# Relational layers of a graph network: scores, score weights and first value weights made while the rows are turned

## The reference, cut to what matters

```python
xr = jnp.einsum('nd,rdf->rnf', x, W)              # values of every relation
oi = xr[etype, dst]; oj = xr[etype, src]
alpha = jax.nn.leaky_relu(oi @ q + oj @ k, 0.2)
m = jax.ops.segment_max(alpha, dst, num_segments=n_nodes)
e = jnp.exp(alpha - m[dst])
z = jax.ops.segment_sum(e, dst, num_segments=n_nodes)
a = e / (z[dst] + 1e-16)
out = jax.ops.segment_sum((a[:, :, None] * oj.reshape(-1, heads, out_ch)).reshape(-1, heads * out_ch), dst, num_segments=n_nodes) + b
```

## Time and profile before

| | |
|---|---|
| median of the runs | 2976.41 us |
| the profiled execution: its time, its span | 2970.5 us, 2968.8 us |
| mean granted TensorE clock | 0.913 of full speed |
| PE, DVE, ACT, GpSimd busy | 2536.1, 2106.1, 1315.0, 310.4 us |
| layer 1: turning, scan, attention begin at | 1202.2, 1214.4, 1448.2 us |
| layer 2: turning, scan, attention begin at | 1866.6, 1879.1, 2096.8 us |

### The profile page before, as it was taken

How to read it: one execution, slowest core, us unless ns; L and a number is a source line. 1 busy time by engine, 2 the same in 40 slices (tenths; PEclk the granted TensorE clock), 3 DMA queues, 4 the chain that set the end, 5 groups by cost and what they waited for, 6 DMA issues and landing times. The chain is left out here.

```text
span 2968.8 us, 39008 instructions
## 1 busy us (share of the span) xinstructions
PE 2536.1 (85%) x14382; PEld 2118.7 (71%) x14383; DVE 2106.1 (71%) x3030; ACT 1315.0 (44%) x1649; POOL 310.4 (10%) x166
## 2 busy tenths in 40 slices
PE   6877894888856994799699999699999979998888
PEld 3556892232323994699699999599888769896668
DVE  6775899999974555699689988660567687136555
ACT  1573225989831000222578776221565563222431
POOL 0000000000003794000000000331000000000013
PEclk9997656999976997899899999899999999999989
DMA  2467542611104554455646643452634362311012
GB/s 69 131 174 180 150 150 67 237 52 35 35 33 178 189 197 158 154 180 160 201 121 181 170 118 90 150 171 81 187 122 129 102 194 70 85 54 59 1 41 80
DMA packets 174702, 366.47 MB, mean 123 GB/s; under 512 B 24871, under 2 KB 103541, under 8 KB 174034
## 3 DMA queue, kind: packets, MB, share of 16 engines
q1 hardware_dynamic: 122024, 274.54, 30.9%
q10 hardware_dynamic: 49312, 73.97, 7.4%
q0 software_dynamic: 3200, 15.73, 1.5%
HBM read 281.06 MB, written 83.12 MB: 123 GB/s over the span
## 5 line engine op out<-in xcount | busy, mean ns | idle before, releaser
L1649 PE MATMUL gat_acc<-far_u,gat_ft 125*65 125x512 f32 x720 | 286.3, 538 | 58.1 <-DVE far_u L1717 57.6
L2246 PE MATMUL rg_out<-rg_w,rg_hT 128*125 128x256 f32 (+1 forms) x900 | 276.6, 307 | 8.0 <-POOL rg_w L1185 8.0
L2247 PE MATMUL rg_out<-rg_w,rg_hT 128*125 128x256 f32 (+1 forms) x900 | 275.5, 306 | 0.0
L2248 PE MATMUL rg_out<-rg_w,rg_hT 128*125 128x256 f32 (+1 forms) x900 | 275.3, 306 | 0.0
L1649 PEld LDWEIGHTS gat_acc<-far_u,gat_ft 125*65 125x65 f32 x720 | 93.7, 142 | 246.9 <-issue 153.6
L2246 PE MATMUL rg2a_acc<-rg2a_value_part,rg2a_wts_part 125*125 125x512 f32 x600 | 204.8, 341 | 14.8 <-DVE rg2a_wts_part L1958 11.4
L2247 PE MATMUL rg2a_acc<-rg2a_value_part,rg2a_wts_part 125*125 125x512 f32 x600 | 205.5, 342 | 0.0
L2248 PE MATMUL rg2a_acc<-rg2a_value_part,rg2a_wts_part 125*125 125x512 f32 x600 | 203.8, 340 | 0.0
L1684 ACT ACTIVATE far_u<-gat_rows,gat_ks 125x1250 f32<-125x1250 f32 x118 | 156.7, 1328 | 41.8 <-PE gat_acc L1649 32.7
L2246 PEld LDWEIGHTS rg_out<-rg_w,rg_hT 128*125 128x125 f32 x900 | 169.1, 188 | 8.2 <-issue 8.0
L1697 DVE TENSOR_TENSOR far_u<-far_u,gat_lowb 125x1250 f32<-125x1250 f32 x120 | 174.4, 1454 | 0.4 <-PEq L711 0.4
(11 more groups left out here) (531 smaller groups left out, 6369.3 us busy)
## 6 DMA issues: line engine op xcount, KB each, us to landing
rg2a_values<-values_dram SPq DMA_DIRECT2D x89, 384.0 KB, 3.2
rg1a_counts<-counts_dram SPq DMA_DIRECT2D x26, 820.3 KB
rg_mask<-far_dram SPq DMA_DIRECT2D x60, 312.5 KB, 3.2
moe_raw<-in_L_ffn_w SPq DMA_DIRECT2D x16, 1152.0 KB, 6.9
relw_chunk<-in_L_gnn_W ACTq DMA_DIRECT2D x36, 384.0 KB, 3.1
gat_rows<-rows_dram SPq DMA_DIRECT2D x10, 1250.0 KB, 5.7
sorted_dram<-gat_zeros SPq DMA_DIRECT2D x30, 384.0 KB, 8.9
values_dram<-rg_stage ACTq DMA_DIRECT2D x90, 128.0 KB, 2.9
```

The costliest lines, as they stand in the source:

```text
L1649: last = pe.matmul(acc[h % 2][0:WIDTH, b, 0:c1 - c0], ft[:, t, h, :], wts[i % HB][:, c0:c1], start=(t == 0), stop=(t == NT - 1))
L2246: pe.matmul(out, still[0], moving[0], start=first, stop=False)
L2247: pe.matmul(out, still[0], moving[1], start=False, stop=False)
L2248: return pe.matmul(out, still[1], moving[0], start=False, stop=final)
```

## The change

The scores of both layers move from the scan stage into the turning stage: PE makes group 0 behind the turning of tile 5, group 1 behind that of tile 9, and group 2 last. The scores take three PSUM banks, so the turning has two pairs of banks in place of three. The split of the score weights (DVE), the loads of the first value weights and the bias (ACT's queue), the high part of the first value weights (ACT, behind tile 7) and their low part (DVE, behind the last tile) move there as well; in layer 2 the low part so goes from GpSimd to DVE, and both halves of relation 0 are loaded. In layer 1 the scan stage begins on ACT with the load of the second piece of weights; `LOW_AT` begins at scan 6, not 8. In both layers ACT keeps the shifts ahead of its copy of the step, not behind it. ROOM is 80. Layer 1 needs one semaphore more.

```diff
-    ROOM = 40
+    ROOM = 80
...
-LOW_AT = tuple(range(8, 120, 14))[0:8]
+LOW_AT = tuple(range(6, 120, 14))[0:8]
...
@@ greatest @@
             if score_of:
-                if in_parts:
-                    pe.wait_ge(weights_split, 2)
-                for j, (t0, t1) in enumerate(groups):
...
-                last.then_inc(turned, 1)
-
                 pe.wait_ge(copied, 3)
...
             if other:
                 other.load(act)
-            act.wait_ge(turned, 1)
+            if not score_of:
+                act.wait_ge(turned, 1)
...
@@ RelationValues @@
-    def load(self, act):
+    def load_first(self, act):
         self.load_piece(act, 0)
         act.dma_start(self.bias[:, :], rows_of(self.b, P, 0, D)).then_inc(self.bias_in, 16)
-        self.make_high(act, 0)
+
+    def load(self, act):
+
+        act.wait_ge(self.low, 1)
+        self.load_piece(act, 1)
...
+            if n == steps - 4:
+                self.keep_late(act)
             act.wait_ge(self.made, n + 1)
...
             if n >= 1:
                 send(n - 1)
-            if n == steps - 4:
-                self.keep_late(act)
...
@@ WideRelationValues @@
-        for k in range(len(self.halves)):
...
+        for k in range(1, len(self.halves)):
+            self.make_low(pool, k)
...
+            if n == steps - 8:
+                self.keep_late(act)
             act.wait_ge(self.made, n + 1)
...
-            if n == steps - 8:
-                self.keep_late(act)
...
@@ turn_in_parts @@
-        banks = [[s.ps(f"{tag}_turn{i}{j}", [128, 512]) for j in range(2)] for i in range(3)]
+        banks = [[s.ps(f"{tag}_turn{i}{j}", [128, 512]) for j in range(2)] for i in range(2)]
...
         @block.tensor
         def _(pe):
+            def scores(j):
+                t0, t1 = GROUPS[j]
+                if j == 0:
+                    pe.wait_ge(ends_set, 2)
+                    pe.wait_ge(weights_split, 2)
+                pe.wait_ge(low_out, 2 * t1)
+                out = scores_ps[:, j, 0:(t1 - t0) * (TP + 1)]
+                for c in range(KC):
+                    last = three(pe, out, [x[:, c, :] for x in weight_parts],
+                                 [x[:, c, t0:t1, :].rearrange("p t n -> p (t n)") for x in parts], c == 0, c == KC - 1)
+                last.then_inc(scores_made, 1)
+
             for t in range(NT):
-                if t >= 3:
-
-                    pe.wait_ge(low_out, 2 * (t - 2))
-                turn_tile(pe, g, banks[t % 3], h, t, turned)
+                if t >= 2:
+
+                    pe.wait_ge(low_out, 2 * (t - 1))
+                turn_tile(pe, g, banks[t % 2], h, t, turned)
+                if t in (5, 9):
+                    scores(t // 4 - 1)
+            scores(2)
...
         @block.scalar
         def _(act):
+            values.load_first(act)
             for t in range(NT):
...
+                if t == 7:
+                    values.make_high(act, 0)
...
         @block.vector
         def _(dve):
+            dve.tensor_copy(weight_parts[0][:, :, :], flat).then_inc(weights_split, 1)
+            dve.wait_ge(weights_split, 1)
+            dve.tensor_tensor(weight_parts[1][:, :, :], flat, weight_parts[0][:, :, :].bitcast(F32),
+                              op=ALU.subtract).then_inc(weights_split, 1)
...
+            values.make_low(dve, 0)
             dve.wait_ge(low_out, 2 * NT)
```

More of the change, by code:

```diff
@@ L710, in greatest @@
     MB = 4
+    score_of = scores_made is not None
     with ExitStack() as ctx:
@@ L722, in greatest @@
         mask = [s.sb(f"{tag}_mask{i}", [P, N], BF16) for i in range(MB)] if mask_of else None
-        turn_ps = s.ps(f"{tag}_turn", [2 * CH if score_of else CH, 3, 512])
+        turn_ps = scores_made if score_of else s.ps(f"{tag}_turn", [CH, 3, 512])
         score_ps = s.ps(f"{tag}_score_ps", [TP, 512]) if score_of else None
[L725 to L729, removed]
+        STEP = TP + 1 if score_of else TP
+        scored, scores_out = s.sem(f"{tag}_scored"), s.sem(f"{tag}_scores_out")
         turned, copied, low_done = s.sem(f"{tag}_turned"), s.sem(f"{tag}_copied"), s.sem(f"{tag}_low_done")
@@ L1060, in __init__, with open @@
         self.pieces = [(r, a) for r in range(R) for a in range(self.COUNT)]
+    def open(self, s):
+        self.out_ps = [s.ps(f"{self.tag}_out{i}", [TP, 512]) for i in range(4)]
+        return self
     def load_piece(self, act, k):
@@ L1166, in __init__, with open, make_high, make_low @@
         self.halves = [(r, a) for r in range(R) for a in range(2)]
+    def open(self, s):
+        self.out_ps = [s.ps(f"{self.tag}_out{i}", [TP, 512]) for i in range(4)]
+        return self
+    def make_high(self, act, k):
+        act.wait_ge(self.raw_in[k % 2], k // 2 * 16 + 16)
+        if k >= 2:
+            act.wait_ge(self.made, (k - 1) * NT)
+        act.activation(self.w_parts[k % 2][0][:, :, :], self.raw[k % 2][:, :, :], ACT.Copy).then_inc(self.high, 1)
+    def make_low(self, engine, k):
+        engine.wait_ge(self.high, k + 1)
+        engine.tensor_tensor(self.w_parts[k % 2][1][:, :, :], self.raw[k % 2][:, :, :],
+                             self.w_parts[k % 2][0][:, :, :].bitcast(F32), op=ALU.subtract).then_inc(self.low, 1)
     def load_half(self, act, k):
@@ L2750, in rgat_layers @@
                         parts = [sm.sb(f"{tag}_hT{j}", [128, KC, NT, TP + 1], FR) for j in range(2)]
+                        values = RelationValues(sm, g, tag, parts, w, b1, bias_all, early)
+                        scores_ps = sm.ps(f"{tag}_scores", [2 * R * H, 3, 512])
                         normalize(g, "rg_ln", g.x, h, None, stats=g.row_stats)
-                        turn_in_parts(g, f"{tag}_parts", h, parts)
+                        turn_in_parts(g, f"{tag}_parts", h, parts, weights[layer], scores_ps, values)
@@ L2753, in rgat_layers @@
                         row = [free[:, j * N:(j + 1) * N] for j in range(6)]
-                        greatest(g, tag, H, H, row, lambda r, t: far_tile(g, r, t), ks, qd, ks_low, shifted,
-                                 (lambda c, a, b: [x[:, c, a:b, :].rearrange("p t n -> p (t n)") for x in parts], weights[layer]),
-                                 lambda sc: RelationValues(sc, g, tag, parts, w, b1, bias_all, early),
-                                 [x[:, :] for x in early.lowb], early, single_rows=True)
+                        greatest(g, tag, H, H, row, lambda r, t: far_tile(g, r, t), ks, qd, ks_low, shifted, values.open,
+                                 [x[:, :] for x in early.lowb], early, single_rows=True, scores_made=scores_ps)
@@ L2758, in rgat_layers @@
                     else:
                         parts = [sm.sb(f"{tag}_hT{j}", [128, KC, NT, TP + 1], FR) for j in range(2)]
-                        turn_in_parts(g, f"{tag}_parts", h, parts)
+                        stage = [free[:, 4 * N + j * D // 2:4 * N + (j + 1) * D // 2] for j in range(4)]
+                        values = WideRelationValues(sm, g, tag, parts, w, b2, bias_all, stage, early)
+                        scores_ps = sm.ps(f"{tag}_scores", [2 * R * H, 3, 512])
+                        turn_in_parts(g, f"{tag}_parts", h, parts, weights[layer], scores_ps, values)
@@ L2761, in rgat_layers @@
                         row = [free[:, j * N:(j + 1) * N] for j in range(2)]
                         junk = [free[0:TP, (2 + j) * N:(3 + j) * N] for j in range(2)]
-                        stage = [free[:, 4 * N + j * D // 2:4 * N + (j + 1) * D // 2] for j in range(4)]
                         greatest(g, tag, H, H, [x.unsqueeze(1) for x in row], lambda r, t: far_tile(g, r, t),
-                                 ks, qd, ks_low, shifted,
-                                 (lambda c, a, b: [x[:, c, a:b, :].rearrange("p t n -> p (t n)") for x in parts], weights[layer]),
-                                 lambda sc: WideRelationValues(sc, g, tag, parts, w, b2, bias_all, stage, early), junk,
-                                 early_unit=early)
+                                 ks, qd, ks_low, shifted, values.open, junk, early_unit=early, scores_made=scores_ps)
```

50 lines of the change are left out of this document (15 added, 35 removed).

## The result

Over 20 runs each, the changed kernel takes 2964.88 us and the kernel before 2972.93 us (medians): ratio 0.9973, 95% interval [0.9963, 0.9984], so 8.0 us faster (4.8 to 11.0). The forecast was 8.3 us faster (its 2968.1 us stood on three runs of the kernel before, at 2976.41 us). The size came out right by luck, by errors that cancel: the front of layer 1 lost 4.6 us where 1.3 had been reckoned, and layer 2 gained 11.1 us where 8.0 had been reckoned.

What follows compares the result with a forecast made beforehand. No engine bounds the whole; layer 1's scan stage ends on DVE, layer 2's is PE's. The terms +1.3 - 4.0 - 8.0 + 2.4 gave -8.3 us, from a median of 2976.41 to 2968.1 us, range 2960 to 2976.

Steps and rivals of the forecast that it cites:

- Turning stage: Both layers' turning stages: end at +22.2 us in layer 1 and +23.1 in layer 2, then a 0.45 boundary, PE last.
- Front of layer 1: +1.3: Layer 1's scan stage: scores' write held behind masks and counts, first scan 4.6 us later, fifth scan 1.3 us later.
- Keeping: -4.0: End of layer 1's scan stage: ACT keeps the turned shifts at 1424.65, not 1428.65, so exponentials come 4.0 us sooner.
- Layer 2: -8.0: Layer 2's scan stage: values start at 1892.9, not 1900.88 after GpSimd's low part, and the end follows, 8.0 us sooner.
- Clears: +2.4: Stage boundaries with ROOM 80: five semaphore clears for three, each 1.2 us above an ordinary boundary, 2.4 us slower.
- The write isn't held: Rival, layer 1's front: the scores' write lands early, first scan at +9.05, -14.1 us in all, 2962.3 us; chance 0.12.
- Half clock: Rival, turning stages: scores run at 1.2 GHz, 0.42 us a product, costing 8.8 us a layer, 2985.7 us; chance 0.08.
- Gains don't arrive: Rival: turning 1 or 2 us longer per layer, or layer 1's stage ends on ACT's last send; 2973.1 us, chance 0.20.

Runs made afterwards that it cites:

- e1: The kernel before with ROOM = 80 and nothing else, so five boundaries clear the semaphores, not three; ratio 1.0011, 3.3 us slower.
- e2: The kernel before with ACT keeping the settled shifts ahead of its wait for the value step, in both layers; ratio 0.9985, 4.5 us faster.
- e6: Layer 1 as in the kernel before, layer 2 as in the changed kernel, ROOM = 40 with three clears; ratio to before 0.9969, 9.2 us faster.
- e7: e6 with e2's earlier keeping of the shifts in layer 1; ratio to before 0.9937, median 2957.29 us.
- e10: The kernel before with PE turning tile 9 three times more ahead of the scores, in both turning stages; ratio 0.9994, 1.8 us faster.
- e5: The changed kernel with layer 1's SP queue reordered: mask 0, scores' write, rows 0 to 3, other masks and rows, counts last; ratio to before 0.9956.
- e3: The changed kernel with ROOM = 40 and one unused semaphore left out, so three clears, not five; ratio to before 0.9966, 10.1 us faster.
- e8: The changed kernel, layer 1: scores' write first, then mask 0 and rows, counts last; ACT's second value-weight load behind its scores copy; ratio to before 0.9959.
- e4: The changed kernel with the write of layer 1's scores issued on GpSimd's queue, not SP's; ratio to before 0.9957, 12.8 us faster.
- e11: e7 with e10's extra turning of the last tile in layer 1 only; ratio to before 0.9951.

## Why the prediction came out right

By the table, with all profiles of a form: the changed front costs layer 1 4.6 us up to the turned shifts (225.4, mean of two, against 220.8, mean of before, e1, e2, e6, e7). Keeping first saves 3.3 (end less turned shifts: 22.4, mean of ten, against 25.7, mean of before, e1, e6, e10). Layer 2 saves 11.1 (192.0, mean of ten, against 203.0, mean of before, e1, e2). The clears cost 2.3. That is 4.6 - 3.3 - 11.1 + 2.3 = -7.5 us, and -8.0 was measured. The forecast had +1.3 - 4.0 - 8.0 + 2.4: its path was right in all four terms, two of them were 3 us off, and that these two went opposite ways is luck. Point by point:

- **Turning stage.** Right: 22.9 and 24.3 us long against 22.65 and 23.55 with the boundary, PE last, DVE's low of the weights at +19.8 in layer 1 (1217.80 + 1.75), waits under 1 us. Layer 2's 24.3 has a late clock in it: the granted clock rose 9.9 us into the stage, in the nine other profiles after 4.3 to 6.8, and their stages took 22.7 to 23.3.
- **Front of layer 1: +1.3, measured +4.8** at the fifth scan (48.0, mean of two, against 43.2, mean of five), 4.6 at the turned shifts. The mechanism, a small write held by the masks and counts issued ahead of it, is shown by e5, which leaves one mask of them ahead and puts the first rows next. The sizes were all too low: 9.4 and 8.7 us in flight for 7.85, 5.0 and 4.8 for the first row instead of 3.9, 7.3 from first to fifth scan instead of 6.9. The 3.9 had been taken off a measured 4.65 because no load would compete; without that load it took 5.0, and the seven profiles of the old layer 1, with the load, have 4.65 to 5.70, so the 4.65 was itself their low end. The old layer 1 itself had its fifth scan at 42.0 to 44.1, so 1 us of any single difference is chance.
- **Keeping: -4.0, measured -3.3.** The exponentials do begin 4.0 us sooner; the second rows, which now bind, take 0.7 to 0.8 back (3.70 us from the first to the second exponential in the changed kernel, 3.85 in e2, 3.05 before).
- **Layer 2: -8.0, measured -11.1.** This is the step that failed in size. The sum was made against an execution whose score products ran at full clock. In e1 and e2 the first 11 and 13 of them ran at half, which made the scores 2.1 and 2.6 us longer (12.6 and 13.1 us from the first product to the copies, 10.5 before), and PE turned its shifts at 204.2 instead of 200.7. What makes up the rest of the 3.5 isn't settled; in e1 the scores also begin 0.9 us later. The prediction asked whether the *new* scores might run at half clock and put 8.8 us on it; the same question about the *old* ones was open in its own rows, for layer 1's old scores had eight slow products behind 3 us of idle PE. The change takes that idle time away, and thus a cost that the profile of before happened not to show in layer 2. e10 confirms it: without the idle time all the products are fast. By where the values start (25.8, mean of ten, against 36.3, mean of before, e1, e2), 8.0 of the 10.5 us are PE's wait for GpSimd's low part, 7.92 to 7.97 us in every profile of the old layer 2. So, by this estimate, 8.0 us come from the weights made early and 2.6 from the scores; a run with the weights alone would part the two, and none was made.
- **Clears: +2.4, measured 2.3.**
- **Rivals.** "The write isn't held" is refuted. "Half clock" is refuted for the new scores: of 36 and 18 products a layer, the first two or three are slow in one layer each of the changed kernel, e3 and e8, where the clock had not yet risen (9.6 to 9.9 us into the stage), none in the other fourteen stages of this form. "Gains don't arrive" was right for the keeping by 0.7 us and wrong on the turning.
- **The Trainium skill** (DMA: Bandwidth & Descriptors, Queues, rings and completion order) has one queue's descriptors worked off in ring order. The trace of e4 agrees in direction: the write that left SP's ring landed after 6.6 instead of 9.4 us. But of the 7.4 us above an undisturbed 2.0 it took away 2.8, so the ring alone doesn't explain the rest; what else is in flight on the 16 engines is the cause left, by argument only, unless GpSimd's queue is itself slower; no run here tests that queue alone.

Not settled: why e10's and e11's gain within the stages (5.8 and 1.7 us) doesn't appear in their ratios, and what moves the untouched first 1190 us by up to 9 us from one execution to the next. The intervals, 3 to 5 us either way, leave room for the missing gains without a cause.

## What to carry to other kernels

Work moved ahead of a stage boundary pays only as far as its consumer's first *transfer* comes sooner: when the scores were early, the order on the queue (four masks and counts ahead of a small write) became the limit, and putting the write and the first rows first was worth another 5 us by the ratios, 7 within the stage. A forecast off one profile inherits that execution's clock: look at each stretch behind some microseconds of idle PE, and ask what it would be at the other level, before and after. And take a change apart: here one layer's edit and a moved copy (e7) beat the whole.

## What the runs showed of the hardware

- The same code, behind the same 3.0 to 3.7 us of idle PE, ran its first 7 to 14 score products at 1.2 GHz in seven of eight stages (both of before, e1 and e2, layer 1 of e6 and e7), and all 54 at 2.4 GHz in the eighth (layer 2 of before, 3.0 us idle). In layer 2 the slow products cost 2.1 and 2.6 us. With PE idle for 1.0 or 1.1 us instead, none of three stages had slow ones (e10's two, e11's first).
- An all-engine barrier that clears the semaphores costs 1.14 and 1.17 us above one that doesn't (e1); its clearing instruction takes 0.78 us.
- GpSimd's low parts of layer 2, which now run beside the first scans, slow those down. DVE after:

```profile
1897.80 1.46 DVE L918 CUSTOM_DVE_ANT_0 rgat_h<-rgat_h,rg_mask 125x1250 f32<-125x1250 f32 x1 [6.42 <-DMA rgat_h<-rows_dram]
1899.19 0.08 DVE L918 DVE_READ_ACCUMULATOR2_ANT rg_most<- 125x1 f32 x1
1899.19 6.42 DVE L918 CUSTOM_DVE_ANT_0 rgat_h<-rgat_h,rg_mask 125x1250 f32<-125x1250 f32 x1
```

and GpSimd after:

```profile
1898.61 5.68 POOL L1165 TENSOR_TENSOR rg_w<-rg_raw,rg_w 128x2304 fp32r<-128x2304 f32 x1 [8.74 <-ACT rg_w L1161]
```

The second scan takes 6.42 us instead of 1.46, ending 1.3 us behind GpSimd's instruction, as if it had begun only then. GpSimd's own 5.68 us are 0.65 more than the 5.03 of before, and 0.65 us is what it shares with the first scan (1898.61 to 1899.26). The Trainium skill (SBUF — State Buffer, SBUF: two separate sides) calls the port pair that VectorE and GpSimd share an exclusive lock, held for a whole instruction when VectorE's has two SBUF inputs and GpSimd's reads SBUF; the trace agrees with both numbers. It costs nothing here, since PE binds layer 2.
